# Weights of the gated feed-forward block prepared on GpSimd, in thirds, across the attention batches

## The reference, cut to what matters

```python
# x, ctx: (16, 256, 256) f32; 16 heads of 16
x = x + tanh(g_xattn) * attention(layernorm(x), ctx, ctx, Wq, bq, Wk, bk, Wv, bv, Wo, bo)
x = x + tanh(g_ffn) * ffn(layernorm(x))

def lpbq_dequant(w):                      # blocks of 32 along the input dimension
    wb = w.reshape(O, I // 32, 32)
    s = maximum(max(abs(wb), -1, keepdims=True) / 7, 1e-12)
    return (clip(round(wb / s), -8, 7) * s).reshape(O, I)

def act_qdq(x):                           # one scale for the whole tensor
    s = maximum(max(abs(x)) / 32767, 1e-12)
    return clip(round(x / s), -32768, 32767) * s

def ffn(x):                               # w_gate, w_up: (768, 256); w_down: (256, 768)
    x    = act_qdq(x)
    up   = act_qdq(x @ lpbq_dequant(w_up).T)
    gate = act_qdq(x @ lpbq_dequant(w_gate).T)
    gate = act_qdq(gate * fixed_qdq_u16(sigmoid(gate)))
    return act_qdq(gate * up) @ lpbq_dequant(w_down).T
```

## Time and profile before

| | us |
|---|---|
| three runs | 651.97, 653.18, 654.5 (median 653.18) |
| the profiled execution | 655.12 |
| its span, first to last instruction | 653.3 |
| PE busy | 567.2 (87%) |
| DVE busy | 500.0 (77%) |
| ACT busy | 433.3 (66%) |
| POOL busy | 177.1 (27%) |

### The profile page before, as it was taken

One profiled execution on the slowest core, in us unless ns is written; L12 is line 12 of the kernel. 1 busy time (PEld: TensorE's weight loads), 2 busy tenths in 40 slices (PEclk: granted clock), 3 DMA queues, 4 the chain that ended last, 5 costly groups with the idle time before them and its releaser, 6 DMA issues. The chain is left out here.

```text
span 653.3 us, 11449 instructions
## 1 busy us (share of the span) xinstructions
PE 567.2 (87%) x4271; PEld 340.4 (52%) x4271; DVE 500.0 (77%) x790; ACT 433.3 (66%) x610; POOL 177.1 (27%) x193
## 2 busy tenths in 40 slices
PE   0579999999999999999824988868999989949997
PEld 0345566666666666664323443333444434428886
DVE  3567778999999999888845499994888799964441
ACT  2216787778777778777731345357999898859860
POOL 4412235565555655543550000001000000010000
PEclk9988999999999999999975999897999999979999
DMA  6221344444443544432233000000000000022443
GB/s 212 69 73 51 82 120 133 134 136 132 122 126 117 140 136 122 109 107 63 70 103 112 1 2 1 1 0 1 0 1 1 0 1 1 1 64 81 140 136 97
DMA packets 42182, 48.98 MB, mean 75 GB/s; under 512 B 10384, under 2 KB 29456, under 8 KB 42128
## 3 DMA queue, kind: packets, MB, share of 16 engines
q1 hardware_dynamic: 40976, 44.07, 23.5%
q0 software_dynamic: 1152, 4.19, 2.3%
HBM read 24.51 MB, written 8.65 MB: 51 GB/s over the span
## 5 line engine op out<-in xcount | busy, mean ns | idle before, releaser
L654 DVE TENSOR_REDUCE negm<-s_ps 128x2 f32<-128x512 f32 x256 | 163.6, 682 | 35.2 <-PE s_ps L390 34.8
L549 ACT ACTIVATE pt<-st_ps 128x512 f32<-128x512 f32 x256 | 138.8, 596 | 52.7 <-PE st_ps L405 51.7
L935 PE MATMUL pairs<-xq,wut 128*128 128x512 f16 x576 | 127.7, 384 | 2.6 <-ACT lnall L1100 2.6
L935 PEld LDWEIGHTS pairs<-xq,wut 128*128 128x128 f16 x576 | 56.6, 99 | 71.9 <-issue 6.9
L390 PE MATMUL s_ps<-kst,qst 96*128 96x256 f16 x512 | 80.5, 277 | 9.1 <-DMA kst<-qk 5.1
L405 PE MATMUL st_ps<-qst,kst 97*128 97x512 f16 x256 | 77.0, 382 | 0.8 <-ACT pt L549 0.8
L372 PE MATMUL pv_ps<-pt,vt 128*32 128x256 f32 x1024 | 68.5, 385 | 1.4 <-ACT ot L506 0.7
L935 PE MATMUL pairs<-xq,wgt 128*128 128x512 f16 x288 | 66.4, 390 | 0.0
L1352 POOL PARTITION_ALL_REDUCE vmax<-vmax x5 | 3.3, 673 | 228.8 <-DVE vmax L1178 135.3
L390 PEld LDWEIGHTS s_ps<-kst,qst 96*128 96x128 f16 x512 | 47.2, 98 | 29.7 <-DVE negm L654 16.6
L1009 PE MATMUL pairs<-wdt,h 128*128 128x256 f16 x384 | 48.6, 278 | 9.5 <-ACT h L1138 9.5
(11 more groups left out here) (160 smaller groups left out, 999.3 us busy)
## 6 DMA issues: line engine op xcount, KB each, us to landing
qst<-qk SPq DMA_DIRECT2D x96, 64.0 KB, 2.1
kst<-qk SPq DMA_DIRECT2D x48, 128.0 KB, 3.5
xt<-in_x SPq DMA_DIRECT2D x16, 256.0 KB, 4.2
ct<-in_ctx SPq DMA_DIRECT2D x16, 256.0 KB, 3.8
recb<-rec_dram SPq DMA_DIRECT2D x16, 256.0 KB
xr<-in_x SPq DMA_DIRECT2D x16, 256.0 KB, 4.0
out<-y SPq DMA_DIRECT2D x16, 256.0 KB, 4.3
lnall<-out POOLq DMA_DIRECT2D x8, 512.0 KB, 4.3
```

The source lines that it names most:

```text
L549: nc.scalar.activation(pt[:, (j // 2) % 2, j % 2, kt], st_ps[u % 3][:], ACT.Exp, scale=1.0 / (WS * WS * HD ** 0.5)).then_inc(exp_done, 1)
L654: nc.vector.tensor_reduce(negm[:, b % 2, tt, lo:lo + 5:4], s_ps[tt][:], AX.X, ALU.max, negate=True).then_inc(max_done, 1)
L935: mm = nc.tensor.matmul(ps[:, p, k, :], w[:, a, dt, f * P:(f + 1) * P], xq[:, b, c, dt, :], start=n == 0, stop=n == len(terms) - 1)
```

## The change

The three weights now come transposed from DRAM as well (`w_gate_t`, `w_up_t`, `w_down_t`, inputs laid out on the host side as such), so their elements need no turning. The natural copies are still loaded, but only to take block maxima. DVE makes 48 reciprocals and 48 scales per partition from them (`block_scales(i)`, one step before the steps 2, 34 and 66 of `SCALES`); PE turns this 128x96 tile, ACT copies it to `sct`, SP stores it to DRAM (`sc_dram`) and loads it back twice per weight, as `binv` and `bmul`, each element repeated over the 32 partitions of its block: two DMAs of 384 KB each per table for `w_gate` and `w_up`, six of 128 KB for `w_down`. All weight arithmetic is then on thirds of 128x512: POOL divides, ACT rounds to int16, DVE clips, POOL multiplies back, ACT makes the high part, POOL the low part, straight into `wgt`, `wut` and `wdt`. POOL has a piece at steps 7 and 0 modulo 8 until 27 are done (steps 7 to 111); ACT and DVE follow at steps 3 and 4 modulo 8. The feed-forward part loses its weight work on all engines.

```diff
+    SCALES = (2, 34, 66)
+    PARTS = 3
@@ SP, prologue
-            sp.dma_start(wstage[:].rearrange("p (f d) -> p f d", d=D),
-                         t["w_gate"].rearrange("(f p) d -> p f d", p=P)).then_inc(wn_loaded, 16)
@@ SP, helpers and the loop over g (last in a step)
+            def load_turned(i):
+                sp.dma_start(wt[i].rearrange("p (k o) -> p k o", o=wo_dims[i]),
+                             t[WEIGHTS[i] + "_t"].rearrange("(k p) o -> p k o", p=P)).then_inc(wt_loaded[i], 16)
+            def load_scales(i, kind, to, done):
+                o = wo_dims[i]
+                src = sc_dram[kind * NBLK * P:(kind + 1) * NBLK * P].rearrange("(k v o w) -> k v o w", v=4, o=1, w=o)
+                for k in range(NW // o):
+                    sp.dma_start(to[:, k * o:(k + 1) * o], src[k].broadcast_to((4, BLOCK, o))).then_inc(done[i], 16)
...
+                    if g == at0 - 12:
...
+                        sp.dma_start(wn.rearrange("p (f d) -> p f d", d=(D, D, F)[i]),
+                                     t[WEIGHTS[i]].rearrange("(f p) d -> p f d", p=P)).then_inc(wn_loaded, 16)
+                    if g == at0 - 6:
...
+                        load_turned(i)
+                    if g == at0 + 1:
...
+                        sp.wait_ge(sc_taken, i + 1)
+                        sp.dma_start(sc_dram.rearrange("(c q) -> c q", q=P), sct[:]).then_inc(sc_written, 16)
+                    if g == at0 + 2:
+                        sp.wait_ge(sc_written, 16 * (i + 1))
...
+                        load_scales(i, 0, binv, inv_loaded)
+                    if g == at0 + 3:
...
+                        load_scales(i, 1, bmul, mul_loaded)
@@ PE
+                    pe.wait_ge(sc_taken, sum(w < g for w in SCALES))      # before K's projection
...
-                    for k in range(2):
-                        turn_weights(2 * (g - PREP - 11) + k)
+                if g in SCALES:
+                    i = SCALES.index(g)
+                    pe.wait_ge(blk_ready, 2 * (i + 1))
...
+                    nc.tensor.transpose(bank(g - 2)[0:2 * NBLK, 0, 0:P], sc[:].rearrange("p a k -> p (a k)"), ident[:]
+                                        ).then_inc(sc_turned, 1)
@@ ACT
+                if g in SCALES:
...
+                    nc.scalar.copy(sct[:], bank(g - 2)[0:2 * NBLK, 0, 0:P]).then_inc(sc_taken, 1)
+                for i, n in pieces_behind(g, 3):
...
+                        nc.scalar.copy(wi[:, at0:at0 + WP], wt[i][:, at0:at0 + WP]).then_inc(w_rounded, 1)
...
+                        nc.scalar.copy(kept[i][:, 0, at0:at0 + WP], wt[i][:, at0:at0 + WP]).then_inc(w_high, 1)
@@ POOL
+                if (x := piece(g)) is not None:
...
+                        nc.gpsimd.tensor_tensor(part, part, binv[:, at0:at0 + WP], ALU.mult).then_inc(w_divided, 1)
...
+                        nc.gpsimd.tensor_tensor(part, part, bmul[:, at0:at0 + WP], ALU.mult).then_inc(w_real, 1)
...
+                        nc.gpsimd.tensor_tensor(kept[i][:, 1, at0:at0 + WP], part, kept[i][:, 0, at0:at0 + WP], ALU.subtract
+                                                ).then_inc(w_low, 1)
@@ feed-forward, DVE (PE's turn_weights, ACT's weights_high and keep_weights, SP's two loads go too)
-                if c == 1:
-                    block_scales(0)
-                if c == 2:
-                    to_integers(0)
-                if c == 3:
-                    from_integers(0)
-                if c == 4:
-                    block_scales(1)
-                if c == 5:
-                    low_weights(0)
-                    to_integers(1)
-                if c == 6:
-                    from_integers(1)
...
-            low_weights(1)
```

More of the change, by code:

```diff
@@ L125, in attention @@
         bs = sb("bs", [P, NBLK], F32)
-        bi = sb("bi", [P, NBLK], F32)
-        bf = sb("bf", [P, NBLK], F32)
-        wq = sb("wq", [P, 2, NW], F16)
+        sc = sb("sc", [P, 2, NBLK], F32)
+        sct = sb("sct", [2 * NBLK, P], F32)
+        wo_dims = (F, F, D)
+        kept = [t[n][:].rearrange("p a t f -> p a (t f)") for n in ("wgt", "wut", "wdt")]
         s_ps = [pb(f"s_ps{i}", [P, 2, S], F32) for i in range(2)]
@@ L155, in attention @@
         wn_loaded = sem("wn_loaded")
+        wt_loaded = [sem(f"wt_loaded{i}") for i in range(3)]
         blk_max = sem("blk_max")
         blk_scaled = sem("blk_scaled")
-        blk_inv = sem("blk_inv")
-        w_int = sem("w_int")
+        blk_ready = sem("blk_ready")
+        sc_turned = sem("sc_turned")
+        sc_taken = sem("sc_taken")
+        sc_written = sem("sc_written")
+        inv_loaded = [sem(f"inv_loaded{i}") for i in range(3)]
+        mul_loaded = [sem(f"mul_loaded{i}") for i in range(3)]
+        w_divided = sem("w_divided")
+        w_rounded = sem("w_rounded")
         w_clipped = sem("w_clipped")
@@ L227, in before, with piece, pieces_behind @@
             return min(max(-(-(g - off) // PAIRS), 0), NB)
+        def piece(g):
+            b, j = divmod(g - 7, PAIRS)
+            n = 2 * b + j
+            return divmod(n, 3 * PARTS) if j < 2 and 0 <= n < 9 * PARTS else None
+        def pieces_behind(g, j):
+            return [x for x in (piece(g - j - 1), piece(g - j)) if x is not None] if g % PAIRS == j else []
         def bank(g):
@@ L350, in turn_tops @@
                 mm.then_inc(top_turned[hf], 1)
[L352 to L362, removed]
             def values(b, u):
@@ L513, in tops @@
                 nc.scalar.activation(mrow[:, hf, :], frm[0:8, 0, :], ACT.Copy, scale=1.0 / MS).then_inc(top_done[hf], 1)
[L515 to L518, removed]
             act.wait_ge(w_loaded, 48)
@@ L576, in _ @@
                     nc.scalar.activation(woh[:], wof[:], ACT.Copy, scale=WS).then_inc(wo_high, 1)
[L577 to L582, removed]
+                if g in SCALES:
+                    i = SCALES.index(g)
+                    act.wait_ge(sc_turned, i + 1)
+                    if i:
+                        act.wait_ge(sc_written, 16 * i)
+                    nc.scalar.copy(sct[:], bank(g - 2)[0:2 * NBLK, 0, 0:P]).then_inc(sc_taken, 1)
+                for i, n in pieces_behind(g, 3):
+                    at0 = n % PARTS * WP
+                    if n // PARTS == 0:
+                        act.wait_ge(w_divided, PARTS * i + n + 1)
+                        if i:
+                            act.wait_ge(w_clipped, PARTS * (i - 1) + n + 1)
+                        nc.scalar.copy(wi[:, at0:at0 + WP], wt[i][:, at0:at0 + WP]).then_inc(w_rounded, 1)
+                    if n // PARTS == 1:
+                        act.wait_ge(w_real, PARTS * i + n % PARTS + 1)
+                        nc.scalar.copy(kept[i][:, 0, at0:at0 + WP], wt[i][:, at0:at0 + WP]).then_inc(w_high, 1)
         @block.vector
@@ L1420 @@
         "w_gate": L0_ffn_w_gate, "w_up": L0_ffn_w_up, "w_down": L0_ffn_w_down,
+        "w_gate_t": np.asarray(L0_ffn_w_gate).T, "w_up_t": np.asarray(L0_ffn_w_up).T, "w_down_t": np.asarray(L0_ffn_w_down).T,
     }
```

178 lines of the change are left out of this document (54 added, 124 removed).

## The result

The changed kernel takes 702.6 us (median of 4 runs, 699.35 to 703.75), the kernel before 653.67 beside it: a ratio of 1.0725, 95% interval 1.0687 to 1.0762. It is slower, as forecast, by twice as much: 49 us where I had 24, and outside my range of 652 to 690.

The account below looks back on a forecast made before the run. PE was taken to set the pace in attention, DVE in the gate stage. 655.1 - 14.0 (feed-forward gain) + 37.4 (attention's cost) = 678.5 us, 676.6 at the median, said as 677; range 652 to 690.

Parts of the forecast that it names:

- What bounds it, and the sign: Whole kernel: PE sets attention's pace, DVE the gate stage's; the change makes it slower, chance 0.80.
- The feed-forward part: From the gate stage on: DVE loses its weight work, gain 14.0 us, bounds 12 and 15.
- Attention, stall by stall: PE's added waits for keys and tops: 2.2 at the start, 7.1, twice 7.6 and twice 4.2 us.
- The first step that failed: Steps 8, 40, 72: keys in place 11.85 us after the first table's issue, late by 7.1, 7.6 and 7.6 us.
- The second table: Steps 44 and 76: it stands ahead of the reciprocals' store, SP waits, the tops come 4.2 us late each time.
- The second step that failed: Attention beside the tables: first plain loads 2.2 us, DVE's scales up to 3.4 us, about 2.3 lost by PE at step 66.
- The third: Attention: the clock drops to its lower level behind stalls; three drops count, 4.5 us in all.
- All engines are used: Rival: tables use all DMA engines, 2.2 us of data each; 653.7 us, chance 0.15.
- Attention has room: Rival: SP's slack covers the tables, only DVE's block and the first load cost, 5 us; 644 us, chance 0.09.
- The backlog carries on: Rival: SP's delay behind the second table makes the next batch's keys late too, 12 us more; 689 us, chance 0.12.

Follow-up runs that it names:

- e2: The changed kernel without both tables; POOL multiplies each third by itself, so other weights are computed: 658.41 us, ratio 1.0048 to the kernel before.
- e7: Against e2, the six plain loads of weights cut in halves and issued behind xr or the denominators' load: 649.83 us, ratio 0.9934 to the kernel before.
- e8: Against e2, only the first matrix's plain loads kept, those of the other two left out: 651.46 us, ratio 0.9962 to the kernel before.
- e12: Against e8, DVE's block of scales also left out for the second and third matrix: 647.59 us, ratio 0.9891 to the kernel before.
- e1: Against the changed kernel, tables loaded by one DMA per 32 partitions, source outer count 32 in place of 4: 671.23 us, ratio 1.023 to the kernel before.
- e3: Against the changed kernel, the second table issued one step later, behind xr, in its old form: 702.13 us, ratio 1.071 to the kernel before.
- e4: Against the changed kernel, first table issued behind the keys and first tops, second right behind it, old form: 703.1 us, ratio 1.0706 to the kernel before.
- e5: Against the changed kernel, tables with outer count 32, table and plain-load halves spread a batch-half apart, POOL's pieces two batches later: 656.34 us, ratio 1.0035.
- e11: Against the changed kernel, outer count 32, table halves mostly behind the denominators' load, plain-load halves behind xr, scales' block in four pieces: 651.91 us, ratio 0.9948.
- e6: Against e5, same placement but tables in their old form with an outer count of 4: 674.48 us, ratio 1.0304 to the kernel before.

## Why the prediction was wrong in size

*What bounds it, and the sign.* Right. PE's waits for keys and tops are where most of the time went, and the chances had slower at 0.80.

*The feed-forward part.* 14.0 predicted, 12.3 measured, within the bounds; and this stretch differs by up to 2.3 us between runs that have the same code there. Step by step, from the start of the part (352.40 and 413.29): DVE's last maximum ends at 81.6 us, before at 89.3, a gain of 7.7 for 8.8. The chain after:

```profile
493.74 1.14 DVE cmax L1183
...
496.62 2.85 ACT lnall L1057
...
514.87 2.75 ACT lnall L1057
```

The 1.1 that is missing lies in the first chunk: its first maximum starts 17.0 us after the start of the part and not 16.0, for PE's first products ran at the lower clock for longer (0.50 to 422, 8.7 us after the start; before to 360, 7.6 us). From the last maximum to ACT are 1.7 us for 3.2 before, 1.5 gained (1.6 predicted); from ACT's start to its third pass 18.25 for 20.4, 2.1 gained (2.4); the rest 1.0 (1.4).

*Attention, stall by stall.* In excess of what stood before, PE's waits were, with the forecast in brackets: step 0 2.8 (2.2); step 8 11.0 (7.1); step 40 9.6 (7.6); step 72 10.9 (7.6); step 44 3.7 (4.2); step 76 3.8 (4.2); and four that I had not: 0.90, 1.31, 1.40 and 2.71 at 103.13, 131.13, 141.27 and 226.00. Together 48.1 for 32.9. Ahead of the last three of these four stands a plain load of 768 KB each: `w_up` at 123.23 ahead of the tops of step 28, `w_up_t` at 132.07 ahead of the keys of step 32, `w_down` at 216.98 ahead of the tops of step 60. Without any table (e2) the two waits for tops are still 1.31 and 1.80 us.

*The first step that failed* is the term "the keys are in place 2.75 + 8.1 + 1.0 = 11.85 us after the table's first issue". Measured 13.6, 13.5 and 14.1 (69.68 to 83.29, 157.06 to 170.51, 250.99 to 265.10), 5.6 us too little in all. The 8.1 is right in its rate (98 to 103 GB/s), but I summed latency and data of one table as if nothing else lay on those four engines. The keys' and the context's loads, 256 KB issued at 66.86 among them, are the likely company; no run took them away, so the cause of this excess stays open. Before that came the store of the scales: I took its landing as 1.6, from the reciprocals', and so had the table 1.7 to 1.8 us behind the last DMA of `stack_q`. It was 3.6 us at step 8 and 3.4 at step 72, and 1.9 at step 40. The median landing of the store over the three is twice what I took:

```profile
sc_dram<-sct SPq DMA_DIRECT2D x3, 48.0 KB, 3.2
```

Table and store are 9.2 us together, which is what the waits at steps 8, 40 and 72 came out higher.

*The second table.* This step held. I had the second table ahead of the store of the reciprocals, SP waiting for that store until 20.1 us behind the first table's issue (207.4 to 227.5), and the tops 4.2 us late. Measured are 21.3 us (157.06 to 178.34) and 22.6 (250.99 to 273.56), and 3.7 and 3.8 for the tops. SP stood 8.3 us for the landing, from the end of the last `ot` DMA:

```profile
162.87 4.25 SPq L344 DMA_DIRECT2D rec_dram<-rec  x1
167.22 2.76 SPq L349 DMA_DIRECT2D ot<-ot  x4
178.34 0.66 SPq L354 DMA_DIRECT2D recb<-rec_dram  x1
```

In total SP waited for this store as follows, and before not at all:

```profile
SPq L354 <- DMA rec_dram<-rec: 14.9, 4, 8.3
```

What I had not foreseen is that SP is also held while it issues: with both tables under way, this store took 4.25 us to issue where it takes 0.43. That the ring of one slow engine is full and holds the whole queue would fit, but no run shows it by itself.

*The second step that failed* is what I had attention pay beside the tables. I priced the six plain loads at 2.2 us in all, for the first; e7 and e8 show some 7. A load of 768 KB ahead of the keys or of 4 KB of tops is 2 us of every engine each time, and 2.2 at 364 GB/s was there to be counted again for the others. DVE's blocks, counted as a hidden 2.3, cost 1.6 to 2.3 each (e8, e12).

*The third is the clock.* I had 4.5 us, three stalls at 1.5. PE's busy time in attention grew by 11.5. After the stall at step 8 the clock is at half up to 87 us:

```profile
83.00:87.00 4.00, 3.71 (x23) 1.35 (x24) 1.29 (x2) 1.59 (x3) 2.12 (x3) 0.50 0.26 102
87.00:90.00 3.00, 3.00 (x23) 2.10 (x20) 1.29 (x2) 1.53 (x4) 0.68 (x1) 0.73 0.26 101
```

that is 4 us at half and 3 at 0.73: 2.0 + 0.8 = 2.8 us lost for this one stall. There are five stalls of 3.7 us or more behind step 0, and at each of them the clock is at 0.50 when PE starts again or within 2 us of it. That all 11.5 us are the clock's is not shown by a run of its own.

So of the 23.5 us that attention took beyond the forecast, 9.2 are the keys behind tables and store, 5.4 the three waits behind plain loads and 7.0 the clock; the rest are small waits.

*The rivals.* "All engines are used", given 0.15, is refuted by the DMA share. But e1 is the kernel that it describes, and there I had 653.7 for what measured 671.2; it would have been wrong by omissions of the same kind, among them the plain loads and the blocks. "Attention has room" was wrong. "The backlog carries on", 0.12 and 689 us, hardly came: of the waits in the batches that follow, 0.90 us for the keys of step 16 is the only one that has no plain load ahead of it, and e2 has 0.44 there. The range ended too low, since its upper bound took my four main prices as known and only asked whether one more stall came.

## What to carry to other kernels

Before a broadcast is put in a shared queue, count the outermost dimension of its source: 4, 8 and 32 gave a quarter, half and all of the engines, and writing the same transfer the other way was worth 31 us of 49 here, for one changed loop. Then price what is queued behind it, every load of the change and not only the first; a slow transfer moved behind the load that waited for it comes back at the next one (e3, e4), and only shorter pieces, on all engines and far apart (e5, e11), took it away; the same places in the old form (e6) left 3%. And where an engine's stream gets a new wait on a DMA, check what of the old work stands behind it on that engine.

## What the runs showed of the hardware

The rate of such a broadcast grows with the engines up to eight and hardly beyond: 98 to 104 GB/s on four (89 with the 128 KB pieces of `w_down`), 203 on eight, 215 to 237 on sixteen (e1, 157 to 159), so 25 GB/s an engine with four or eight and 13 to 15 with all. A plain load had 364 at full share. And a queue that has two tables on four engines under way holds SP at its next DMA: `xt` took 4.10 us to issue and the reciprocals' store 4.25, where a DMA of this kind took 0.43 elsewhere, and the six DMAs of a table 7.25 where the six before them took 3.61.
